# Quarter-array matmuls for a forward transform and an evaluation at Toom-Cook nodes

## The reference, cut to what matters

```python
def _L0_conv_ref(input, weight, alpha):          # 3x3, 64 -> 64, padding 1
    sign = jnp.where(weight >= 0, 1.0, -1.0)
    return conv(input, sign * alpha)

def _L1_conv_ref(x, w_in, w_dw, fft_filt, w_out):
    h = jnp.einsum('oc,bchw->bohw', w_in, x)      # 64 -> 256 channels
    f = jnp.fft.rfft2(patches_8x8(h)) * fft_filt  # filter by channel and frequency
    h = from_patches(jnp.fft.irfft2(f, s=(8, 8)))
    h = depthwise_conv_3x3(h, w_dw)
    x1, x2 = jnp.split(h, 2, axis=1)
    g = jax.nn.gelu(x1, approximate=False) * x2
    return jnp.einsum('oc,bchw->bohw', w_out, g)  # 128 -> 64 channels
```

## Time and profile before

| | |
|---|---|
| median of 3 runs | 5494.31 us (5494.24 to 5495.86) |
| span of the profiled execution | 5491.0 us, 3.3 us under that median; its own device time is not listed apart from the span |
| busy: PE, DVE, ACT, POOL | 5361.6, 4649.5, 3769.3, 4641.4 us |
| weight loads (PEld) | 3472.6 us |
| granted TensorE clock, mean | 0.997 of full speed |
| DMA | 217.59 MB, mean 40 GB/s |

### The profile page before, as it was taken

The page is one execution under the profiler, slowest core; times in us unless marked ns, Lnnn a source line. Parts: engine busy times, 40 slices in busy tenths (PEclk is TensorE's granted clock), DMA queues, the critical chain, the costliest instruction groups (busy, mean ns, idle before and its releaser), DMA issues.

```text
span 5491.0 us, 174549 instructions
## 1 busy us (share of the span) xinstructions
PE 5361.6 (98%) x75428; PEld 3472.6 (63%) x75428; DVE 4649.5 (85%) x5703; ACT 3769.3 (69%) x4866; POOL 4641.4 (85%) x2727
## 2 busy tenths in 40 slices
PE   5999999999999999999999999999999999999998
PEld 4666666666666666666666666666666666666665
DVE  6889888888888888888888888888889888888876
ACT  3767767676676766767667676676767767676676
POOL 3888888898888988889888888888888888888898
PEclk9999999999999999999999999999999999999999
DMA  2011010110101111011010100101011010110000
GB/s 101 18 49 42 36 43 28 52 39 36 53 22 49 39 38 52 19 53 38 36 52 22 56 32 36 56 36 42 32 49 39 36 42 32 49 42 19 23 21 29
DMA packets 43848, 217.59 MB, mean 40 GB/s; under 512 B 5366, under 2 KB 6104, under 8 KB 36952
## 3 DMA queue, kind: packets, MB, share of 16 engines
q1 hardware_dynamic: 43096, 206.42, 9.8%
HBM read 103.64 MB, written 102.76 MB: 38 GB/s over the span
## 4 chain that ended last, share of the span: by engine, by line
PE 89%; DVE 7%; issue 2%; POOL 0%; ACT 0%; DMA 0%; SPq 0%; DVEq 0%; POOLq 0%; ACTq 0%
PE PS L952 27%; PE PS L970 21%; PE PS L912 14%; PE PS L941 11%; PE PS L984 6%; PE PS L930 6%; PE PS L921 4%; DVE hf L690 3%; DVE v L697 2%; DVE bn L628 1%; DVE g L722 1%; DVE PS L713 0%; DVE PS L706 0%; POOL v_lo L357 0%; DMA alpha_sb<-in_alpha 0%
## 5 line engine op out<-in xcount | busy, mean ns | idle before, releaser
L357 POOL TENSOR_TENSOR v_lo<-v,v_hi 128x1024 f16<-128x1024 f32 (+1 forms) x1792 | 3354.1, 1896 | 496.3 <-ACT v_hi L487 496.3
L697 DVE TENSOR_TENSOR v<-PS,smul 128x1024 f32<-128x1024 f32 (+1 forms) x1792 | 1915.4, 1087 | 425.6 <-PE PS L952 226.5
L487 ACT ACTIVATE v_hi<-v 128x1024 f16<-128x1024 f32 (+1 forms) x1792 | 1652.1, 944 | 706.8 <-DVE v L697 554.0
L952 PE MATMUL PS<-hf,c_nodes 64*128 64x512 f32 (+1 forms) x7168 | 1696.1, 574 | 7.1 <-DVE v L697 3.7
L970 PEld LDWEIGHTS PS<-c_ext,v_hi 128*128 128x128 f16 x14336 | 1128.7, 97 | 477.4 <-issue 289.3
L970 PE MATMUL PS<-c_ext,v_hi 128*128 128x100 f16 (+2 forms) x14336 | 1256.6, 203 | 5.1 <-ACT gel L507 3.4
L970 PE MATMUL PS<-c_ext,v_lo 128*128 128x100 f16 (+2 forms) x14336 | 1248.2, 202 | 0.0
L970 PEld LDWEIGHTS PS<-c_ext,v_lo 128*128 128x128 f16 x14336 | 1116.9, 97 | 1.2
L690 DVE TENSOR_TENSOR hf<-PS,mult 128x1024 f32<-128x1024 f32 (+1 forms) x896 | 954.8, 1086 | 85.1 <-PE PS L941 64.2
L952 PEld LDWEIGHTS PS<-hf,c_nodes 64*128 64x128 f32 x7168 | 570.6, 185 | 473.8 <-issue 125.3
L912 PE MATMUL PS<-S_hi,csign 64*64 64x448 f16 (+2 forms) x8640 | 738.7, 338 | 9.4 <-POOL S_lo L346 9.4
(11 more groups left out here) (74 smaller groups left out, 6243.4 us busy)
## 6 DMA issues: line engine op xcount, KB each, us to landing
out_x<-Xa SPq DMA_DIRECT2D x96, 448.0 KB, 2.5
out_x<-Xb SPq DMA_DIRECT2D x96, 448.0 KB, 2.5
Xa<-in_x SPq DMA_DIRECT2D x8, 2240.0 KB, 9.1
Xb<-in_x SPq DMA_DIRECT2D x8, 2240.0 KB, 8.8
Xa<-in_x SPq DMA_DIRECT2D x8, 1792.0 KB, 6.8
Xb<-in_x SPq DMA_DIRECT2D x8, 1792.0 KB, 7.0
Xa<-in_x SPq DMA_DIRECT2D x8, 1344.0 KB, 5.9
Xb<-in_x SPq DMA_DIRECT2D x8, 1344.0 KB, 6.0
```

The costliest lines, as they stand in the source:

```text
L357: nc.gpsimd.tensor_tensor(v_lo[:, img, :, k0:k1, :], v32[:, V_BUF[kind(b, s)][img][grp], :, 0:k1 - k0, :], v_hi[:, img, :, k0:k1, :], ALU. ...
L487: nc.scalar.activation(v_hi[:, img, :, k0:k1, :], v32[:, V_BUF[kind(b, s)][img][grp], :, 0:k1 - k0, :], ACT.Copy).then_inc(act_vhi[img], 1)
L697: nc.vector.tensor_tensor(v32[:, V_BUF[kind(b, s)][img][grp], :, 0:k1 - k0, :], PS[:, bank:bank + 2, 0:(k1 - k0) * C2].rearrange("p i (k c ...
L952: last = nc.tensor.matmul(PS[:, bank + side, 0:(k1 - k0) * C2], c_nodes[half, :], hf[half, img, k0:k1, :].rearrange("p k c -> p (k c)"), s ...
```

## The change

Both `forward_transform` and `evaluated` issue four matmuls where they issued two. Each takes 64 of the 128 weight columns, and so writes 64 of the 128 output partitions: in the forward transform one image's channels, in the evaluation the lower or upper 64 nodes. The order of the quarters is that of the convolution. Moving operands, banks, waits and the semaphore increment on the last matmul stay as they are.

```diff
             def forward_transform(n, s, bank):
                 pe.wait_ge(act_xT, n * STRIPS + s + 1)
                 for k in range(NBLK):
-                    for side in range(2):
+                    for side, img in ((0, 0), (1, 1), (0, 1), (1, 0)):
                         half = slice(side * P * P, (side + 1) * P * P)
-                        last = nc.tensor.matmul(PS[:, bank + side, k * P * P:(k + 1) * P * P], xT[half, k, :], c_fwd[half, :],
-                                                start=True, stop=True)
+                        last = nc.tensor.matmul(PS[img * C:(img + 1) * C, bank + side, k * P * P:(k + 1) * P * P],
+                                                xT[half, k, img * C:(img + 1) * C], c_fwd[half, :], start=True, stop=True)
                 last.then_inc(pe_xf, 1)
...
                 k0, k1 = GROUPS[grp]
                 pe.wait_ge(dve_hf, 4 * (b * STRIPS + s) + HF_ORDER[kind(b, s)].index(grp) + 1)
-                for side in range(2):
+                for side, upper in ((0, 0), (1, 1), (0, 1), (1, 0)):
                     half = slice(side * P * P, (side + 1) * P * P)
-                    last = nc.tensor.matmul(PS[:, bank + side, 0:(k1 - k0) * C2], c_nodes[half, :],
+                    points = slice(upper * 64, (upper + 1) * 64)
+                    last = nc.tensor.matmul(PS[points, bank + side, 0:(k1 - k0) * C2], c_nodes[half, points],
                                             hf[half, img, k0:k1, :].rearrange("p k c -> p (k c)"), start=True, stop=True)
                 last.then_inc(pe_v[img], 1)
```

## The result

The changed kernel takes 5406.2 us (median of 4 runs, 5405.3 to 5407.3), the kernel before 5494.7: a ratio of 0.984, interval 0.9825 to 0.9853. That is 88 us less; 5409 was forecast. The profiled execution spans 5404.5 us.

A forecast was written before the change was run, and what follows sets the result against it. PE was taken to bound stretches between convolution steps, a DVE, ACT and POOL loop the plain ones; 67.5 + 7.2 + 3.3 + 4.5 + 2.6 = 85 us off 5494.3 gives 5409 us; 8 in 10: 5368 to 5465.

The forecast's parts named there:

- between convolution steps: Stretches from one forward transform to the next, between two steps with convolutions: 0.75 us less each, times 90 = 67.5 us.
- after the last convolution step: The stretch behind a pair's last step with convolutions keeps 0.48 us of forward's saving: x15 = 7.2 us.
- into the first one: Stretch into a pair's first convolution step: POOL's up to the evaluation before the convolution; keeps 0.22 us, x15 = 3.3.
- Streaming at no change: Both matmul lines: four quarters running side by side stream their columns in the same time as before; no gain or loss.
- The rival in which quarters of the same rows take turns: Evaluation calls: two fp32 quarters over the same 64 rows alternate, doubling 0.91 us; about 6900 us in full, chance 0.07.
- The load sets forward's pace: Forward transform: 14 weight loads each 0.053 us shorter with 64 columns, 0.74 us off PE's 1.51.
- The pace rival: Forward transform: PE can't issue 56 narrow matmuls and loads faster, so it stays at 1.51 us; 5454 us, chance 0.12.
- The shape change: Evaluation ahead of the convolution, now both 64x64: no drain (0.09) or load (0.03), 0.12 us per convolution step; own load 0.05.
- B waits for the product of A: Evaluations before (A) and after (B) forward: B needs DVE's product of A, so 0.48 of forward's 0.74 us arrives.
- Plain stretches: Stretches without convolutions: forward's saving worth under 0.1 us; 0.05 each for the second evaluation, 90 x 0.05 = 4.5 us.
- the loop: Stretches without convolutions: DVE gate, ACT carry and node rounding, POOL subtraction, DVE product of A, then B; bounds their 20.8 us.
- PE has slack in the plain stretches: Stretches without convolutions: PE's 20.4 us hides a 0.39 us wait for DVE's product before a widening matmul.

The follow-up runs named there:

- The doubled forwards: Every block of the forward transform computed twice: in the changed kernel 5583.8 us, in the kernel before (64x128 forward) 5847.6 us.
- one half of the change alone: Only the evaluation in quarters, the forward transform left 64x128, against the kernel before: 5519.6 us, ratio 1.0044.
- forward alone: Only the forward transform in quarters, the evaluation left 64x128, against the kernel before: 5441.3 us, ratio 0.990.

## Why the prediction was right, point by point

By position in the pair, from the starts of all forward transforms in the two traces:

| stretches | forecast, us | measured, us |
|---|---|---|
| between convolution steps, 90 | -67.5 | -58.6 |
| after the last convolution step, 15 | -7.2 | -7.8 |
| into the first one, 15 | -3.3 | -2.7 |
| plain, 90 in the 15 pairs | -4.5 | -19.2 |
| last pair, 13 | -2.6 | -1.7 |
| start and end of the run | 0 | +3.5 |
| sum | -85 | -86.5 |

The +3.5 at the start and end is no larger than the spread of the kernel before's own runs beside these experiments, 5493.0 to 5497.7 us, and isn't read as an effect of the change.

- **Streaming at no change** held: 608 ns against 623 for the 512-column instruction, and the order of the quarters is free. The rival in which quarters of the same rows take turns is out.
- **The load sets forward's pace** held: 28 loads in 1.51 us were the bound, and a pass of four quarters now takes about 0.059 us, (0.99 - 0.22) / 13 with the record of one matmul, 218 ns, taken off. The doubled forwards weigh the term directly: a whole forward added 1.56 us in the kernel before and a quartered one 0.82, 0.75 less where 0.74 was forecast. Each tile still gets 14 instructions of 64 moving columns; only its weight columns were halved, and with them the partitions that it writes. No run changed one of these two without the other, so that it is the load rests on the load's record, 188 ns before and 135 after. The pace rival is out; so is the 1.4 us that the Trainium skill's page TensorEngine Tiling (Array Packing), section Instruction Overhead, would give for 56 matmuls (an estimate from its 60 cycles each): they start in 0.77 us, 14 ns apart on average. The measurement decides; a small streaming dimension was worth tiling here, as its cost was the load, not the stream.
- **The shape change** held at 0.16 for 0.17, by itself and in the whole.
- **B waits for the product of A** held: 0.50 us measured where 0.48 and A's load of 0.05 were counted. The load was the part that was sized too high: A starts 0.14 us after the last matmul of the interpolation in both kernels, and its product ends only 0.02 earlier. That, and the stops, is what the first row of the table lacks: regular stretches lost 0.71 us rather than 0.75, 64 us for 90, and stops gave some 5 back.
- **Plain stretches** were the weak step: the loop was read in one place, in the last pair, and taken for all. In the second plain stretch of a pair A's product didn't wait for POOL, it waited for PE, like in a convolution step, and was done 0.53 us before B. In the third it did wait for POOL but was done 0.40 us before B. In both, B could come earlier. Before the change, the timelines of DVE and of PE at the start of the second and of the third:

```profile
2490.87 0.69 DVE L697 TENSOR_TENSOR v<-PS,smul 128x512 f32<-128x512 f32 x1 [0.31 <-PE PS L952]
...
2492.09 1.08 PE L952 MATMUL PS<-hf,c_nodes 64*128 64x512 f32 x4
...
2511.97 0.69 DVE L697 TENSOR_TENSOR v<-PS,smul 128x512 f32<-128x512 f32 x1 [0.87 <-POOL v_lo L357]
...
2513.06 1.08 PE L952 MATMUL PS<-hf,c_nodes 64*128 64x512 f32 x4
```

  Those two kinds of stretch, 30 in all, brought 8.1 and 4.8 us of the 19.2. The closeness of the sum is luck in part: 8.9 us were forecast too much between convolution steps and 14.7 too little in the plain stretches.
- **PE has slack in the plain stretches** was half true. PE's wait of 0.39 us for DVE's spectra is real, yet the doubled forward in the kernel before cost 1.53 to 1.57 us in the plain stretches. Outside the two just named, PE came to B less than 0.1 us after it could: the product was done 0.14 us ahead of B (0.06 in the fourth plain stretch), as in the earlier trace rows, and 0.06 is what B needs. So PE could not be slower for free, and being faster brought about 0.1 us. The wait that told this apart isn't but the absence of one ahead of B.

## What to carry to other kernels

Where small fp32 matmuls follow each other with new weights, time the loads before the streams: halving the columns of a load can halve the group, if the tiles run side by side. Count the changes of tile shape in the order of the queue, and convert neighbours together; here one half of the change alone lost time and both together gained more than their sum. And when two chains arrive at a point together, speeding one up brings only its lead over the other, but afterwards an edit to the other chain, which was worthless or worse before, can pay.

## What the runs showed that was not expected

PE can stop in the middle of a run of matmuls without waiting for any semaphore: 0.25 to 3.5 us at a time, five times in the changed kernel, 56 times with twice the quarters in forward, never in mid run in the kernel before or with its own forward doubled. In the doubled kernel 112 matmuls and 112 loads are to go in 1.6 us, 7 ns each. A queue of its own brings the instructions; packets, MB and share of the DMA engines, in the changed kernel and in the one before:

```profile
q8 instruction: 716, 11.73, 0.9%
```

```profile
q8 instruction: 611, 10.01, 0.8%
```

A packet is a block of 16 KB. The change adds 26,880 matmuls and loads, and there are 105 blocks more, one for every 256 of them: this queue carries PE's instructions. Its packets in the trace tie the stops to it. In 86 places of all traces PE stands still for 0.05 us or more between two matmuls of one line, with no semaphore to wait for: 5 in the changed kernel, 3 and 7 with its other orders of quarters and of ScalarE, 2 with forward alone, 69 with the doubled quarters (evaluations and shorter stops counted too), none elsewhere. Every one of the 86 ends 1.2 to 1.65 us after a block has landed, though the blocks come 7 to 8 us apart on average, so that fewer than one in ten would do so by chance. In no trace do blocks land closer than 3.3 us, 13 ns for an instruction, against the 7 that the doubled forward asks for. So PE had most likely run out of fetched instructions; no run changed the fetching itself.

Where a stop falls stays open in part. Three of the changed kernel's five are in one stretch of the pair, from step 9 to step 10, and with the doubled forward that stretch is over 1 us too long in 11 of 15 pairs.
